# A two-layer cross-attention kernel: every attention pair turned by 32x32 blocks and one direct exchange, four score banks, keys and queries spread without a detour

## The reference, cut to what matters

```
# layer 0, attention "A": q from x, k and v from ctx, 16 heads of 64, a mask per batch
x = layernorm(softmax(q k^T / 8 masked) v @ Wo + bo + x) * gamma + beta
# layer 1, 16 heads of 16: "B" attends to x itself with one mask for all, "C" to ctx
x = layernorm(x + softmax(q k^T / 4 masked) v @ o_w + o_b) * g1 + b1
x = layernorm(x + softmax(q k^T / 4) v @ co_w + co_b) * g2 + b2
x = layernorm(x + relu(x @ lin1_w + b) @ lin2_w + b) * g3 + b3
```

## Time and profile before

| | |
|---|---|
| median of three runs | 1823.72 us |
| profiled execution | 1826.15 us |
| its span | 1824.3 us |
| granted TensorE clock, mean | 0.985 |
| busy: TensorE, its weight loads | 94%, 71% |
| busy: VectorE, ScalarE, GpSimd | 70%, 65%, 54% |
| moved by DMA | 324 MB, 178 GB/s |

### The profile page before, as it was taken

One profiled execution on the slowest core, in us unless ns is written; L12 is line 12 of the kernel. 1 busy time (PEld: TensorE's weight loads), 2 busy tenths in 40 slices (PEclk: granted clock), 3 DMA queues, 4 the chain that ended last, 5 costly groups with the idle time before them and its releaser, 6 DMA issues.

```text
span 1824.3 us, 36986 instructions
## 1 busy us (share of the span) xinstructions
PE 1719.5 (94%) x11328; PEld 1287.7 (71%) x11328; DVE 1269.6 (70%) x4778; ACT 1190.3 (65%) x3985; POOL 990.9 (54%) x1030
## 2 busy tenths in 40 slices
PE   7999999999999999999999999999999999998887
PEld 5776677777777677777777777677777777776556
DVE  3465667786868668686776868678686867667763
ACT  3364766667676666767666676766667677566752
POOL 3252655657465464746556474555657565455742
PEclk9999999999999999999999999999999999998899
DMA  7432327585766758576585757658575766613010
GB/s 167 143 106 84 107 67 230 172 273 161 238 204 200 245 170 272 161 244 206 178 266 181 249 159 236 209 181 280 173 251 163 226 223 182 202 59 139 30 58 12
DMA packets 227521, 324.12 MB, mean 178 GB/s; under 512 B 31744, under 2 KB 196352, under 8 KB 219136
## 3 DMA queue, kind: packets, MB, share of 16 engines
q1 hardware_dynamic: 224208, 321.75, 55.5%
q10 hardware_dynamic: 3120, 0.01, 0.1%
HBM read 170.69 MB, written 151.00 MB: 176 GB/s over the span
## 4 chain that ended last, share of the span: by engine, by line
PE 77%; DVE 6%; DMA 5%; ACT 5%; SPq 5%; issue 2%; POOL 0%; POOLq 0%; DVEq 0%
PE ps_g L681 45%; PE ps_t L824 10%; PE ps_t L847 8%; PE ps_s L800 8%; ACT prob L930 3%; PE ps_av L800 3%; DMA prob_b<-p_kept 3%; PE ps_av L847 3%; DVE prob L1105 2%; DMA p_kept<-blocks 2%; SPq L593 1%; PE ps_g L687 1%; DVE res_ln L1081 1%; DVE prob_b L1136 1%; SPq L576 1%
## 5 line engine op out<-in xcount | busy, mean ns | idle before, releaser
L1229 POOL TENSOR_TENSOR prob<-prob,recip 128x512 f32<-128x512 f32 x768 | 788.4, 1049 | 670.5 <-DVE recip L1115 670.4
L930 ACT ACTIVATE prob<-prob,ext 128x256 f32<-128x256 f32 x1536 | 757.2, 499 | 11.7 <-DVE ext L1105 11.5
L940 ACT ACTIVATE prob_t<-ps_t 128x512 f32<-128x512 f32 x384 | 226.3, 594 | 398.1 <-PE ps_t L824 397.3
L824 PE MATMUL ps_t<-ident,prob 128*128 128x128 f32 x1920 | 304.6, 283 | 7.6 <-DVE prob_b L1136 5.4
L930 ACT ACTIVATION_READ_ACCUMULATOR prob<-prob,ext 128x1 f32 x1536 | 295.5, 192 | 0.0
L824 PEld LDWEIGHTS ps_t<-ident,prob 128*128 128x128 f32 x1920 | 216.9, 142 | 94.2 <-issue 51.6
L1105 DVE CUSTOM_DVE_ANT_0 prob<-ps_s,mask_a 128x256 f32<-128x256 f32 x392 | 145.3, 421 | 88.3 <-PE ps_s L800 70.6
L1127 DVE STREAM_TRANSPOSE blocks<-prob 128x512 f32<-128x512 f32 x288 | 183.9, 676 | 3.2 <-POOL prob L1229 2.3
L1105 DVE CUSTOM_DVE_ANT_0 prob<-ps_s,zero 128x256 f32<-128x256 f32 x392 | 144.4, 418 | 45.3 <-PE ps_av L800 37.3
L1105 DVE CUSTOM_DVE_ANT_0 prob<-ps_s,mask_b 128x256 f32<-128x256 f32 x368 | 135.9, 417 | 24.5 <-PE ps_s L800 14.8
L800 PE MATMUL ps_s<-k_ctx,q 64*128 64x256 f32 x784 | 144.8, 402 | 7.3 <-DVE ext L1105 3.0
(11 more groups left out here) (116 smaller groups left out, 2980.9 us busy)
## 6 DMA issues: line engine op xcount, KB each, us to landing
p_kept<-blocks SPq DMA_DIRECT2D x576, 128.0 KB, 2.4
prob_b<-p_kept SPq DMA_DIRECT2D x144, 512.0 KB, 3.4
k_parts_C<-k_hl SPq DMA_DIRECT2D x64, 256.0 KB, 3.1
k_parts_B<-k_hl SPq DMA_DIRECT2D x64, 256.0 KB, 3.1
q_parts_B<-q_hl SPq DMA_DIRECT2D x64, 256.0 KB, 3.5
k_B<-k_parts_B SPq DMA_DIRECT2D x16, 1024.0 KB, 7.6
q_B<-q_parts_B SPq DMA_DIRECT2D x16, 1024.0 KB, 7.7
q_parts_C<-k_hl SPq DMA_DIRECT2D x64, 256.0 KB, 4.7
```

The costliest lines, as they stand in the source:

```text
L824: last = nc.tensor.transpose(two(ps_t[e])[:, kt, qt * P:(qt + 1) * P], src[:, e, qt, kt * P:(kt + 1) * P], ident[:, :])
L930: last = nc.scalar.activation(tile, tile, ACT.Exp, bias=ext[:, slot, e, t:t + 1], scale=-1.0, accum_out=sums[:, slot, e, t:t + 1])
L940: nc.scalar.activation(prob_t[:, e], two(ps_t[e]), ACT.Copy).then_inc(copied_second, 1)
L1229: nc.gpsimd.tensor_tensor(rows, rows, recip[:, slot, e].unsqueeze(2) .to_broadcast([P, TT, TOK]), ALU.mult).then_inc(normed[s], 1)
```

## The change

All 24 pairs of a body, in the filling and draining bodies as well, are now turned by VectorE in blocks, in one instruction a pair of 128x1024, at step "D" of pair g-2. TensorE's transposes "T0" and "T1", ScalarE's and VectorE's copies of them and the step "L" are gone. The four transfers a pair go from `blocks` straight into `prob_b`, in SBUF, without DRAM. For that the keys are numbered otherwise: a key is 128 k + 4 r + g where it was 128 k + 32 g + r, so that the 32 elements of a block, which lay side by side, are read with a step of four elements, 16 bytes. `blocks` is now a ring of two pairs, `prob_b` one of four, `prob` one of three (it was four). The two banks `ps_t` become two more for the scores: four, two a pair; pair g may begin once pair g-2 has been taken, and `ps_av` serves the value products alone.

Keys and queries of B and C are spread in eight transfers of 128 KB, SBUF to SBUF. The keys of C are still kept in DRAM and loaded in two halves. The key buffers `k4` have two copies of the head dimension, in each of which one half is zero, so that one product of all 128 rows and 512 columns gives both heads' scores of 128 queries: two products a pair of B or C instead of four of 64 rows and 256 columns. The jobs "v" are emptied by ScalarE instead of VectorE. The input of the residual is loaded into its own place, and no longer through `x_tok`. Layer norms stay where they were, on VectorE with a part on GpSimd, under new semaphores.

```diff
-P_RING = 4
+P_RING, B_RING, T_RING = 3, 2, 4
-DVE_JOBS = {"q": 4, "v": 4, "kc": 1, "wo": 1,
+DVE_JOBS = {"q": 4, "kc": 1, "wo": 1,
-ACT_JOBS = {"k": 4, "vc": 1, "x1T": 1, "x2T": 1, "x3T": 1, "h": 3}
+ACT_JOBS = {"k": 4, "v": 4, "vc": 1, "x1T": 1, "x2T": 1, "x3T": 1, "h": 3}
...
-        if older(BLOCKS, 0, True):
-            steps.append(("D",) + older(BLOCKS, 0, True))
-        if older(BLOCKS + 1, 0, True):
-            steps.append(("L",) + older(BLOCKS + 1, 0, True))
-        turn = older(LAG, 0, False) or older(LAG, 1)
-        if turn:
-            steps.append(("T0",) + turn)
+        if g - BLOCKS in pairs:
+            steps.append(("D",) + pairs[g - BLOCKS])
         steps.extend(jobs)
...
-        ("A", 0): late + [dma("save k", "B"), job("ks"), dma("save q", "B")],
-        ("A", 1): [dma("k", "B"), job("qs"), ln("ln1"), job("v", 0)],
+        ("A", 0): late + [dma("k", "B"), job("ks"), dma("q", "B")],
+        ("A", 1): [job("qs"), ln("ln1"), job("v", 0)],
...
-        prob_t = sb("prob_t", [P, 2, TT, TOK])
-        blocks = sb("blocks", [P, 4, TT * 2 * TT * SLOT])
-        prob_b = sb("prob_b", [P, 2, 4, TT * 2 * TT * SLOT])
+        blocks = sb("blocks", [P, B_RING, 4, 2 * TT * TT * SLOT])
+        prob_b = sb("prob_b", [P, T_RING, 4, 2 * TT * TT * SLOT])
-        k4 = {s: sb("k4_" + s, [P, PAIRS, TOK], F32R) for s in "BC"}
+        k4 = {s: sb("k4_" + s, [P, 2, PAIRS, TOK], F32R) for s in "BC"}
...
+            def spread_queries(s, b, home):
                 parts = q_hl if s == "B" else k_hl
+                home_free(s, b, home)
                 for part in range(PARTS):
                     if part % 2 == 0:
                         sp.wait_ge((q_high[s], taken["qs" if s == "B" else "qc"])[part // 2], count(b, 1, 1))
+                    for e in range(2):
+                        row = HALF * e + DH1 * part
+                        sp.dma_start(q4[home][row:row + DH1].bitcast(F32), parts[:, part // 2, e]
+                                     ).then_inc(spread_q[s], 16)
+
+            def exchange(body, step):
+
+                n = body.place(step)
                 sp.wait_ge(flipped, n + 1)
+                if n >= T_RING:
+                    (_, s0, p0, _), b0 = body.pair_at(n - T_RING)
+                    sp.wait_ge(weighed[s0], count(b0, QUADS, p0 // 2 + 1))
                 for q in range(4):
+                    sp.dma_start(prob_b[:, n % T_RING, q, :], blocks[q * SLOT:(q + 1) * SLOT, n % B_RING]
+                                 ).then_inc(landed[n % T_RING], 16)
...
+                past = body.earlier(step, 2, lambda x: x[0] == "S")
                 if past:
                     (_, s0, p0, _), b0 = past
+                    pe.wait_ge(masked[s0], count(b0, HEADS, 2 * p0 + 2))
+                if s != "A":
+                    for t in range(TT):
+                        nc.tensor.matmul(two(score_bank(body, step, t)), q[:, t * P:(t + 1) * P], k,
+                                         start=True, stop=True).then_inc(scored[s], 1)
+                    return
...
-                src = prob[:, body.slot(step, P_RING)].rearrange("p e t (k g r) -> p k (e t) g r", k=TT, r=SLOT)
-                out = blocks[:, :, :].rearrange("p g (k x q) -> p k x g q", k=TT, q=SLOT)
-                for kt in range(TT):
-                    last = nc.vector.transpose(out[:, kt], src[:, kt])
-                last.then_inc(flipped, 1)
+                if n >= B_RING:
+                    dve.wait_ge(landed[(n - B_RING) % T_RING], 64 * ((n - B_RING) // T_RING + 1))
+                src = prob[:, body.slot(step, P_RING)].rearrange("p e t (k r g) -> p (e t k) r g", k=TT, r=SLOT)
+                out = blocks[:, n % B_RING].rearrange("p g (m q) -> p m g q", q=SLOT)
+                nc.vector.transpose(out, src).then_inc(flipped, 1)
```

More of the change, by code:

```diff
@@ L158, in schedule @@
     if present == {"x", "a"}:
-        after = {place: [x for x in jobs if x[1:3] not in (("res0", 0), ("load", 0))] for place, jobs in after.items()}
+        after = {place: [x for x in jobs if x[1:3] not in (("res0", 0), ("x_in", 0), ("mask_in", 0))] for place, jobs in after.items()}
         after["A", 0] = [job("k", 1)] + after["A", 0]
-        head += [res("res0", 0), io("load")]
+        head += [res("res0", 0), io("mask_in")]
     if present == {"x"}:
@@ L165, in schedule @@
     steps += here(head)
[L166 removed]
+    line = Line(steps, carried)
     for o in order:
@@ L503, in _, with load_mask @@
         def _(sp):
-            def load(body, step):
+            def load_mask(body, step):
                 b = body.batch(step)
@@ L550, in load_values @@
                              v_kept[bass.ds(b, 1)].rearrange("b p t d -> p b t d")).then_inc(v_loaded, 16)
-            def save_keys(body, step):
-                b = body.batch(step)
-                sp.wait_ge(taken["ks"], count(b, 1, 1))
-                if not (isinstance(b, int) and b == 0):
-                    sp.wait_ge(spread_k["B"], count(b - 1, 16, 16))
-                for part in range(PARTS):
-                    sp.dma_start(k_parts["B"][0, :, part].rearrange("e r c t -> (r c) e t"),
-                                 k_hl[:, part % 2]).then_inc(k_saved["B"], 16)
@@ L571, in save_queries, with spread_keys @@
-            def save_queries(s, b):
+                elif not (isinstance(b, int) and b == 0):
+                    sp.wait_ge(scored[s], count(b - 1, HEADS, HEADS))
+            def spread_keys(b):
+                sp.wait_ge(taken["ks"], count(b, 1, 1))
+                home_free("B", b, "B")
+                for part in range(PARTS):
+                    for e in range(2):
+                        row = HALF * e + DH1 * part
+                        sp.dma_start(k4["B"][row:row + DH1, e].bitcast(F32), k_hl[:, part % 2, e]
+                                     ).then_inc(spread_k["B"], 16)
@@ L932, in exps @@
                     last.then_inc(exped[s], 1)
-            def evac_turned(body, step, e):
-                if step[2] % 2 == 0:
-                    return
-                quad = body.quad(step)
-                act.wait_ge(turned, 2 * (quad + body.turned_so(quad + 1, False)) + e + 1)
-                nc.scalar.activation(prob_t[:, e], two(ps_t[e]), ACT.Copy).then_inc(copied_second, 1)
             def evac_weighed(body, step):
@@ L984, in _ @@
             last.then_inc(own_ready, 1)
+            for s in "BC":
+                for e in range(2):
+                    last = nc.vector.memset(k4[s][HALF * e:HALF * (e + 1), 1 - e].bitcast(F32), 0.0)
+            last.then_inc(halves_cleared, 1)
             dve.wait_ge(w_in["bias0"], 32)
@@ L1095, in extremes @@
                 slot = body.slot(step, P_RING)
+                n = body.place(step)
+                if n >= P_RING:
+                    dve.wait_ge(flipped, n - P_RING + 1)
                 if s == "A" and p == 0:
                     dve.wait_ge(mask_read, count(b, 1, 1))
-                for e in range(2):
-                    value = held(count(b, HEADS, 2 * p + e + 1))
+                for i in range(2):
+                    value = held(count(b, HEADS, 2 * p + i + 1))
                     dve.wait_ge(dve_const, 1)
                     dve.wait_ge(scored[s], value)
-                    for t in range(TT):
+                    for j in range(2):
+                        e, t = (i, j) if s == "A" else (j, i)
                         mask = {"A": mask_a[:, t, :], "B": mask_b[:, t, :],
@@ L1105, in extremes @@
                         last = nc.vector.tensor_tensor_reduce(
-                            out=prob[:, slot, e, t, :], in0=two(score_bank(body, step, e))[:, t, :], in1=mask,
+                            out=prob[:, slot, e, t, :], in0=two(score_bank(body, step, i))[:, j, :], in1=mask,
                             scale=-SCALE[s], scalar=BIG, op0=ALU.add, op1=ALU.min,
```

307 lines of the change are left out of this document (109 added, 198 removed).

## The result

The changed kernel takes 2098.76 us (median of 4 runs, 2096.8 to 2100.64) against 1820.7 us (median of 4, 1815.0 to 1829.72) for the kernel before, measured beside it. The ratio is 1.152, 95% interval [1.147, 1.157]: 15% slower, where 10% faster was forecast and 1940 us was the end of the range. One slip in the diff above: the last added `rearrange` ends in `-> p (e t k) g r` (L1049 of the changed kernel), and not in `r g`.

A forecast was written before the change was run, and what follows sets the result against it. TensorE was taken as the bound, busy 103.6 of 107.2 us a body. Span 1824.3 - 122 (bodies) - 35 (fill) - 25 (drain) = 1642, plus 1.85 around it 1644; less the profiled run's 2.4 excess, 1642 us. Range 1595 to 1940.

The forecast's parts named there:

- I take 676 ns and 512 more elements at 1.0 ns, 1.19 us: VectorE's new 128x1024 turn: one start instead of two, 1.19 us each, 28.5 us a body for 24.
- Rival 1: VectorE's turn reads at half pace, 2.21 us, and VectorE becomes the bound: 1946 us, deciding from 1.78 us; chance 0.25.
- TensorE's work becomes 88.5 us: TensorE in a full body: 103.6 us busy less 15.1 us of transposes taken away.
- the scores, counted at nothing: TensorE's score products of B and C: two of 512 columns assumed to cost the same as four of 256.
- the bounds of -3 and +6.8: Range kept for the new score products of B and C, in us a body on TensorE.
- TensorE alone would need 88.5 and today's 3.6 of idle: Full body as set by TensorE: its remaining work plus the unchanged idle time, 92.1 us.
- The waits for scores I count as gone: VectorE in a full body: no more waiting for scores, since four banks let TensorE be a whole pair ahead.
- the 97.0: Full body as set by VectorE: 89.6 us busy plus waits of 3.3 and 4.1 us, a gain of 10.2.
- The transfers of the exchange are hidden as long as they land before the value products: Exchange in the body: 8.1 us available after the turn, against 2.0 of issue and 2.4 of landing.
- SyncE issues 133 for 87, hidden behind the body, with a rival below: SyncE's queue in a body: more DMA issues, occupied 67 us, counted at no cost.
- Rival 3: Exchange lands too late for VectorE's turns, also behind eight spreads in SyncE's queue: likely 6 us a body, 1744 us; chance 0.09.
- Fill and drain: I count 35 and 25 us: Gains at start and end, each out of 61.5 us of transposes that TensorE loses there.

The follow-up runs named there:

- the repaired kernel: Changed kernel with the turn side by side, key spreads through DRAM, and key order made where key products are emptied: 1883.7 us, ratio to before 1.030.

## Why the prediction was wrong

**What bounds the kernel before** was read rightly: TensorE, at 103.6 of 107.2 us. The run of before with stepped turns supports it: 10 us more on VectorE a body made the body 0.7 us longer.

**"I take 676 ns and 512 more elements at 1.0 ns, 1.19 us."** Without a stride it is right (1222 ns). With the step of 16 bytes that the diff writes, the turn takes 2.04 us. Rival 1 had 2.21 and its bound of 1.78 us was passed; its other sign, VectorE busy above 95%, did not come (842.55 of 960.12 us, 88%), since VectorE waits for DMAs as well. This is the first step that failed, and it is worth 121 to 128 us of the miss. The trace of before had no such row, the diff showed the step, and one rule of the Trainium skill spoke against it. I gave it 25%.

**"TensorE's work becomes 88.5 us."** In the repaired kernel it is 750.35 / 8 = 93.8 us. Part is the scores, counted at nothing. In the changed kernel a pair of C starts at 869.38 and the next job at 869.95, and again at 871.49 and 872.14:

```profile
867.77 1.68 PE L775 MATMUL ps_av<-prob_b,v 128*64 128x256 f32 x14
869.38 0.73 PE L754 MATMUL ps_s<-k_C,q_C 128*128 128x512 f32 x2
869.95 1.89 PE L639 MATMUL ps_g<-x_t,wl 128*128 128x256 f32 x8
871.49 0.82 PE L754 MATMUL ps_s<-k_C,q_C 128*128 128x512 f32 x2
872.14 1.89 PE L639 MATMUL ps_g<-x_t,wl 128*128 128x256 f32 x8
```

That is 0.57 to 0.65 us a pair for 0.43 in the earlier trace rows, 2.2 to 3.5 us a body over 16 pairs, inside the bounds of -3 and +6.8. The rest of the 5.3 us lies in what was taken off. The 121.0 us of the transposes are the busy time of that group alone, 0.63 us for each four, and its last product still runs while the next one starts. In the kernel before, four of them start at 902.96 and the product behind them at 903.49:

```profile
902.96 0.60 PE L824 MATMUL ps_t<-ident,prob 128*128 128x128 f32 x4
```

So four transposes held the engine for 0.53 us and not 0.63, which is 2.4 us a body over its 24 fours. With every product of the eight bodies counted only until the next one starts, the transposes come to 12.8 us a body and not 15.1, and the scores of B and C go from 7.1 to 10.3 us in the repaired kernel.

**"TensorE alone would need 88.5 and today's 3.6 of idle."** The idle time of the bound before is no measure of its idle time after. Once TensorE has less work, it stands for layer norms, for ScalarE and for landings: 8.4 us a body without any exchange, 12.5 with it.

**"The waits for scores I count as gone."** They are not. With four banks VectorE still waits for scores (35.3 + 25.8) / 8 = 7.6 us a body in the repaired kernel and 8.6 without the exchange. In that last run VectorE's work is as forecast (88.9 us for 89.6), but it waits 13.6 us and not 7.4; that is the difference between its body of 102.5 us and the 97.0.

**"The transfers of the exchange are hidden as long as they land before the value products."** Their landing is near the forecast in the median, 2.6 us for 2.4, and up to 9.7 us in the eight bodies; four issues take 2.6 us (823.16) and not 2.0, and the way through turn, issue and landing takes 4.1 us a body that nothing hides.

**"SyncE issues 133 for 87, hidden behind the body, with a rival below."** Rival 3 happened as well, by the part that it gave one sentence: the spreads ahead of an exchange. There are 16 and not 8 in a row, at 0.64 to 0.75 us and not 0.5. The landing of the exchange stays below the rival's bound of 4.9 us in the median; but the exchanges behind the spreads are late twice, in their issue (837.65) and in their landing (5.5 to 7.6 us), and no run tells the two apart. Forecast at 6 us a body; measured 6.3 to 6.6, and 97 to 104 us in all. The rivals were weighed as if only one could come true, and they add up: 128 and 97.

**"Fill and drain: I count 35 and 25 us."** The sign was wrong: +70.6 and +46.7. I counted only engines' work there. What the change adds is a way by DMA in the path of every pair from the first on. In the first body it meets the constants' loads: queued behind them in the changed kernel, and still landing after up to 16 us when it is put between them or in another queue. Without the exchange the fill is 15.7 and the drain 13.0 us shorter than before, so even those terms were half of what I counted. The granted clock was lower too, 0.84 and 0.82 there for 0.99 and 0.94 before, but it stretched TensorE's work little: in the fill the same 1144 product records are busy 212.5 us at 0.87 in the repaired kernel and 206.9 at 0.95 without the exchange.

**The sum** by its own steps, all measured: before 1821; turns moved off TensorE, with the exchange free, 1747 (-74, forecast -182); the exchange +137 (forecast 0), 1884; the stepped read and the direct spreads +215 (with the key order that they spare), 2099. So the steps that failed are a turn put at 1.19 us that takes 2.04, an exchange put at nothing that takes 137 us, spreads put at nothing in the sum that take about 100, and a gain without all of these of 74 us and not 182. The -74 is the work of all the other edits together, the four score banks and the products of 512 columns among them; no run takes these apart, and the run without the exchange is a single one.

## What to carry to other kernels

Where a change moves work from the bound to an engine that is next to it, count the new latency as well as the new busy time, and at the start and the end most of all, where a DMA has no cover and shares the engines with the first loads. Read the step in bytes of every new access pattern: 16 bytes from one element to the next made two readers of SBUF 1.64 and 1.67 times slower here, and was free for ScalarE out of PSUM. Before a queue is given more issues, find the longest run of them that can stand ahead of one that is waited for, and add rivals that don't exclude each other.

## What the runs showed of the hardware that I had not expected

- VectorE's transpose of 128x1024 has a cliff between 8 and 16 bytes of step, 1230 and 2041 ns, and is flat on both sides. TensorE pays for 16 bytes in its moving operand as well, 633 ns for 386 over 256 columns; steps between were not tried on it.
- A spread of 128 KB onto 16 partitions lands after 5.9 us for the keys of B and 7.7 for its queries in the median, and an exchange of 128 KB onto all 128 after 2.6. Both write pieces of 1 KB, but the spreads are issued in rows of 8 and 16, and the exchanges right behind them take 5.5 to 7.6 us too, so that the partitions alone are not shown to be the cause.
- The layer norms' pass over 128x256 takes 414 ns on VectorE in the changed kernel, and 594 to 627 in all its variants whose turn reads side by side:

```profile
L1002 DVE TENSOR_SCALAR res_ln<-res_ln,mv_ln,rstd_ln 128x256 f32<-128x256 f32 x128 | 47.5, 414 | 5.5 <-POOL rstd_ln L1105 5.5
```

```profile
L1002 DVE TENSOR_SCALAR res_ln<-res_ln,mv_ln,rstd_ln 128x256 f32<-128x256 f32 x128 | 71.1, 597 | 5.5 <-POOL rstd_ln L1105 5.5
```

(the changed kernel, and the same one with the turn side by side). In the kernel before it is 652 ns, and 641 with stepped turns, so the step by itself isn't the cause. It stays open.
